# Image, text and weight loads of an early-fusion block: transfers cut at multiples of 16 rows, issued in another order, and the class row spread by transfers

## What is computed

```python
x = data.reshape(b, C, HP, P, WP, P).transpose(0, 2, 4, 1, 3, 5).reshape(b, N, F)   # 16, 36 patches, 768
x = jnp.einsum('bnf,df->bnd', x, W_lin) + b_lin
out = jnp.concatenate([cls, x], axis=1) + position_embeddings                        # 16, 37, 256
h = jnp.concatenate([out, txt], axis=1)                                              # 16, 165, 256
h = h + attn(layernorm(h), Wq, Wk, Wv, Wo)       # 16 heads, 4 key heads, rope, window of 32 to each side
h = h + ffn(layernorm(h), w1, conv_w, conv_b, w2)   # ternary weights, inputs rounded to 8 bits, conv of 3, silu
```

## Time and profile before

| | us |
|---|---|
| median of 3 runs | 399.28 |
| lowest, highest | 397.93, 400.9 |
| span of the profiled execution | 397.3 |
| PE busy in it | 364.4 |
| DVE busy | 306.3 |
| ACT busy | 256.9 |
| POOL busy | 215.4 |

### The profile page before, as it was taken

The page is one execution under the profiler, slowest core; times in us unless marked ns, Lnnn a source line. Parts: engine busy times, 40 slices in busy tenths (PEclk is TensorE's granted clock), DMA queues, the critical chain, the costliest instruction groups (busy, mean ns, idle before and its releaser), DMA issues.

```text
span 397.3 us, 8398 instructions
## 1 busy us (share of the span) xinstructions
PE 364.4 (92%) x3029; PEld 272.9 (69%) x3029; DVE 306.3 (77%) x647; ACT 256.9 (65%) x483; POOL 215.4 (54%) x245
## 2 busy tenths in 40 slices
PE   6599799999999999999989999999999998987885
PEld 2277557877877796678767876787678776843733
DVE  2247659654599889888998698959895997799795
ACT  3213436668786779567868686768677966772552
POOL 5406689689379919892789427972993016000000
PEclk9989999999999999999999999999999999999999
DMA  8781521201100022002000220022012001000101
GB/s 238 167 183 32 167 86 29 54 10 27 26 12 2 2 53 48 19 20 55 18 0 2 60 45 2 2 61 42 12 26 51 19 2 34 4 2 0 35 2 35
DMA packets 21907, 16.71 MB, mean 42 GB/s; under 512 B 12435, under 2 KB 20936, under 8 KB 21865
## 3 DMA queue, kind: packets, MB, share of 16 engines
q1 hardware_dynamic: 20970, 15.11, 15.4%
q10 hardware_dynamic: 895, 1.06, 1.0%
HBM read 9.82 MB, written 3.38 MB: 33 GB/s over the span
## 4 chain that ended last, share of the span: by engine, by line
PE 69%; DVE 14%; ACT 7%; issue 5%; DMA 4%; SPq 1%; DVEq 0%; ACTq 0%
PE bank L1790 8%; PE bank L1870 8%; PE bank L1841 7%; PE bank L1884 6%; PE bank L1943 5%; PE bank L1913 4%; PE bank L1984 4%; PE bank L1944 4%; DMA shared<-in_x 4%; PE bank L1861 4%; PE bank L1737 3%; PE bank L1904 2%; ACT shared L1339 2%; PE bank L1803 2%; PE bank L1893 2%
## 5 line engine op out<-in xcount | busy, mean ns | idle before, releaser
L1502 DVE TENSOR_REDUCE mx<-bank 120x4 fp32r<-120x376 f32 (+3 forms) x88 | 44.0, 506 | 24.5 <-PE bank L1853 24.1
L1274 ACT COPY pT<-bank 94x480 f32<-94x480 f32 (+3 forms) x88 | 48.2, 554 | 21.0 <-PE bank L1870 20.7
L1266 ACT ACTIVATE pr<-bank 120x376 f32<-120x376 f32 (+3 forms) x88 | 39.6, 454 | 28.9 <-PE bank L1861 28.1
L1870 PE MATMUL bank<-cst,pr 120*94 120x120 f32 (+3 forms) x352 | 51.3, 271 | 2.7 <-ACT pr L1266 2.7
L1841 PE MATMUL bank<-kbd,q_hl 128*120 128x376 f32 (+3 forms) x176 | 51.1, 373 | 1.2 <-ACT pT L1274 0.6
L1114 POOL TENSOR_TENSOR rs<-ve,half_neg 110x3 f32<-110x3 f32 x16 | 16.7, 1045 | 63.9 <-DVE ve L1530 47.7
L1943 PE MATMUL bank<-xT_hi,w1T 128*128 128x330 f32 x128 | 44.2, 351 | 1.3 <-DVE late L1585 0.9
L1870 PEld LDWEIGHTS bank<-cst,pr 120*94 120x94 f32 (+3 forms) x352 | 36.1, 122 | 10.4 <-ACT pr L1266 6.4
L1121 POOL TENSOR_SCALAR xn<-h,mv,rs 110x256 f32<-110x256 f32 x21 | 27.6, 1323 | 24.7 <-PE bank L1778 24.4
L1136 POOL TENSOR_TENSOR rc<-qk,cst 110x320 f32<-110x320 f32 x22 | 20.0, 909 | 38.3 <-ACT qk L1237 37.4
L1944 PE MATMUL bank<-xT_lo,w1T 128*128 128x330 f32 x128 | 39.5, 314 | 0.0
(11 more groups left out here) (132 smaller groups left out, 882.6 us busy)
## 6 DMA issues: line engine op xcount, KB each, us to landing
kbd<-shared SPq DMA_DIRECT2D x56, 41.2 KB, 2.1
out<-h SPq DMA_DIRECT2D x7, 330.0 KB
wn<-in_w SPq DMA_DIRECT2D x2, 1024.0 KB, 6.7
shared<-in_x SPq DMA_DIRECT2D x4, 432.0 KB
h<-in_txt SPq DMA_DIRECT2D x1, 770.0 KB
late<-in_lin SPq DMA_DIRECT2D x1, 768.0 KB, 7.1
vw<-v_rows SPq DMA_DIRECT2D x8, 94.0 KB
v_rows<-qk SPq DMA_DIRECT2D x8, 82.5 KB
```

The costliest lines, as they stand in the source:

```text
L1266: nc.scalar.activation(pr[:, g % 3, 0:HKV * WIDTH[j]], S_BANKS[g % 2][0:QP, 0:HKV * WIDTH[j]], ACT.Exp, scale=HD ** -0.5).then_inc(exped, 1)
L1274: nc.scalar.copy(pT[0:WIDTH[j], g % 3, :], S_BANKS[g % 2][0:WIDTH[j], 0:HKV * QP]).then_inc(p_kept, 1)
L1502: nc.vector.tensor_reduce(mx[:, g % 4, :].bitcast(F32R), S_BANKS[g % 2][0:QP, 0:HKV * WIDTH[j]].rearrange("p (k c) -> p k c", k=HKV), axis ...
L1870: o = nc.tensor.transpose(S_BANKS[g % 2][0:w, kv * QP:(kv + 1) * QP], pr[:, g % 3, kv * w:(kv + 1) * w], ident[0:QP, 0:QP])
```

## The change

Four edits.

1. Loads are cut at multiples of 16 rows. An image load becomes two transfers, of 64 and of 8 rows, and its two readers wait for both. The five pieces of text become eight: 64 + 9, 48 + 7, 16 + 2 and 96 + 14 rows.
2. SP issues image load 0, the patch weights, image loads 1 to 3, the text of pair 0, `wqk` and the mask; `wo` and `conv` follow the text of the other pairs. ACT's queue keeps the identity, the class row, the constants and the positions, in this order (positions were second).
3. POOL adds token and position once, for one row, in place in `clsb`. SP spreads the sum to the class rows of all pairs by two transfers with a repeated source, instead of one copy of `h` within `h`.
4. ACT sorts its half of image load 1 ahead of `keep_patch(0)`, no longer behind it.

```diff
--- before.py
+++ after.py
@@ -61,6 +61,7 @@
 LOADS = 4
 PER_LOAD = B // LOADS
 LROWS = PER_LOAD * CH * GRID
+EVEN_ROWS = LROWS // 16 * 16
 KP = CH * PATCH * PATCH // 128
 NTOK = B * NPATCH
 
@@ -740,7 +741,7 @@
     'dve.keep_pix_v': (3, 4, 8),
     'dve.abs_w': (19, 21),
     'dve.ternary': (24, 26, 29, 31, 32, 34),
-    'act.sort_a': (1, 3, 5),
+    'act.sort_a': (3, 5),
     'act.keep_pix_a': (2, 4, 10),
     'act.keep_patch': (6, 11, 26, 28),
     'act.keep_w': (59, 67, 73, 78),
@@ -978,13 +979,16 @@
         txt0 = 1 + NPATCH
         n00 = TT - txt0
         n10 = TT - first2 - txt0
-        TXT_PARTS = [
-            (txt0, txt0 + 64, 0, 0, 0),
-            (txt0 + 64, TT, 0, 0, 64),
+        TXT_RUNS = [
+            (txt0, TT, 0, 0, 0),
             (0, first2, 1, 0, n00),
             (first2 + txt0, TT, 1, 1, 0),
             (0, TT, 2, 1, n10),
         ]
+        TXT_PARTS = []
+        for p0, p1, t, b, r0 in TXT_RUNS:
+            even = p0 + (p1 - p0) // 16 * 16
+            TXT_PARTS += [(p0, even, t, b, r0), (even, p1, t, b, r0 + even - p0)]
 
         def sort_pix(i, lo, hi):
 
@@ -1003,8 +1007,7 @@
             eng.wait_ge(txt_first, 16 * len(TXT_PARTS))
             if n:
                 eng.wait_ge(txt_rest, 16 * len(TXT_PARTS))
-            eng.wait_ge(cls_made, 1)
-            eng.wait_ge(cls_moved, 16)
+            eng.wait_ge(cls_moved, 16 * 2)
             for s in tok_tiles(n):
                 eng.wait_ge(tok_in[s], 16 * len(tok_pieces(s)))
 
@@ -1015,14 +1018,17 @@
             xv = x.rearrange("b c (hp py) w -> (b c hp) (py w)", py=PATCH)
 
             def load_img(i):
-                sp.dma_start(raw[:, i, :], xv[LROWS * i:LROWS * (i + 1), :]).then_inc(img_in[i], 16)
+                for r0, r1 in ((0, EVEN_ROWS), (EVEN_ROWS, LROWS)):
+                    sp.dma_start(raw[r0:r1, i, :], xv[LROWS * i + r0:LROWS * i + r1, :]).then_inc(img_in[i], 16)
 
             load_img(0)
             sp.dma_start(wlT[:, :, :], lin_d).then_inc(wlin_in, 16)
+            for i in range(1, LOADS):
+                load_img(i)
             for p0, p1, t, b, r0 in TXT_PARTS:
                 sp.dma_start(h[p0:p1, 0, t, :], txt_v[b, r0:r0 + p1 - p0, 0, :]).then_inc(txt_first, 16)
-            for i in range(1, LOADS):
-                load_img(i)
+            sp.dma_start(wqk[:, :, :], wqk_d).then_inc(wqk_in, 16)
+            sp.dma_start(mask_sb[:, :], maskbits).then_inc(mask_in, 16)
 
 
             def move_tokens(s):
@@ -1036,10 +1042,13 @@
                 sp.dma_start(w2n[:, :, :], w2.rearrange("(t p) h -> p t h", p=128)).then_inc(w12_in, 16)
 
             sp.wait_ge(cls_made, 1)
-            sp.dma_start(h[first2:first2 + 1, :, 1, :], h[0:1, :, 0, :]).then_inc(cls_moved, 16)
+            for row, t in ((0, 0), (first2, 1)):
+                sp.dma_start(h[row:row + 1, :, t, :], clsb[:, 0:1, :].to_broadcast([1, PAIRS, D])).then_inc(cls_moved, 16)
             move_tokens(0)
             for p0, p1, t, b, r0 in TXT_PARTS:
                 sp.dma_start(h[p0:p1, 1:PAIRS, t, :], txt_v[b, r0:r0 + p1 - p0, 1:PAIRS, :]).then_inc(txt_rest, 16)
+            sp.dma_start(wo_sb[:, :, :], wo_d).then_inc(wts_in, 16)
+            sp.dma_start(conv[:, :, :], conv_d).then_inc(wts_in, 16)
 
             def load_v(n):
                 sp.wait_ge(v_ones, 1)
@@ -1103,8 +1112,7 @@
             nc.gpsimd.memset(ones[:, :], 1.0).then_inc(v_ones, 1)
             nc.gpsimd.memset(kbd[1][:, :, :, :], 0.0).then_inc(kbd_zeroed, 1)
             pool.wait_ge(cls_in, 16)
-            nc.gpsimd.tensor_tensor(h[0:1, :, 0, :], clsb[:, 0:1, :].to_broadcast([1, PAIRS, D]),
-                                    clsb[:, 1:2, :].to_broadcast([1, PAIRS, D]), ALU.add).then_inc(cls_made, 1)
+            nc.gpsimd.tensor_tensor(clsb[:, 0, :], clsb[:, 0, :], clsb[:, 1, :], ALU.add).then_inc(cls_made, 1)
             pool.wait_ge(consts_in, 16)
 
             def rstd(n, var, ve, rs, made, done):
@@ -1192,13 +1200,12 @@
         @block.scalar
         def _(act):
             act.dma_start(cst[:, 0:C_REST], ident_d).then_inc(ident_in, 16)
-            act.dma_start(posb[:, :], pos_d).then_inc(pos_in, 16)
             act.dma_start(clsb[:, :, :], cls_d).then_inc(cls_in, 16)
             act.dma_start(cst[:, C_REST:C_END], consts).then_inc(consts_in, 16)
-            act.dma_start(wqk[:, :, :], wqk_d).then_inc(wqk_in, 16)
+            act.dma_start(posb[:, :], pos_d).then_inc(pos_in, 16)
 
             def sort_pix_act(i):
-                act.wait_ge(img_in[i], 16)
+                act.wait_ge(img_in[i], 16 * 2)
                 if i >= 2:
                     act.wait_ge(pix_turned, 2 * (i - 1))
                 nc.scalar.copy(*sort_pix(i, GRID // 2, GRID)).then_inc(sorted_a, 1)
@@ -1216,11 +1223,9 @@
                     act.wait_ge(tok_in[s - 2], 16 * len(tok_pieces(s - 2)))
                 nc.scalar.copy(tokp[0:rows, s % 2, :], Z_BANKS[s % 2][0:rows, 0:D]).then_inc(tok_kept, 1)
 
-            act.dma_start(mask_sb[:, :], maskbits).then_inc(mask_in, 16)
-            act.dma_start(wo_sb[:, :, :], wo_d).then_inc(wts_in, 16)
-            act.dma_start(conv[:, :, :], conv_d).then_inc(wts_in, 16)
             sort_pix_act(0)
             keep_pix(0)
+            sort_pix_act(1)
             keep_patch(0)
 
             def keep_xn(n, k):
@@ -1381,7 +1386,7 @@
                 for s in work["keep_w"].get(q, ()):
                     keep_ternary(s)
                 for i in work["sort_a"].get(q, ()):
-                    sort_pix_act(i + 1)
+                    sort_pix_act(i + 2)
                 for i in work["keep_pix_a"].get(q, ()):
                     keep_pix(i + 1)
                 for s in work["keep_patch"].get(q, ()):
@@ -1396,7 +1401,7 @@
             nc.vector.tensor_scalar(neg_id[:, :].bitcast(F32R), ident[0:QP, 0:QP], -1.0, None,
                                     ALU.mult).then_inc(neg_made, 1)
             def sort_pix_dve(i):
-                dve.wait_ge(img_in[i], 16)
+                dve.wait_ge(img_in[i], 16 * 2)
                 if i >= 2:
                     dve.wait_ge(pix_turned, 2 * (i - 1))
                 nc.vector.tensor_copy(*sort_pix(i, 0, GRID // 2)).then_inc(sorted_v, 1)
```

## The result

The changed kernel takes 407.14 us (405.64 to 412.57, 4 runs) against 399.62 us (397.93 to 400.9, 4 runs): ratio 1.0158, 95% interval 1.0118 to 1.0198. It is slower by 1.6%: 6.3 us by the ratio, which leaves the slow execution of 412.57 us out, and 7.5 us by the two medians. The forecast was 2.5 us slower, in a range up to 404.6.

The account below looks back on a forecast made before the run. PE bounds the kernel, so only the start of its unbroken run at `turn_pix(2)` counts: +4.0 (positions) − 1.45 (image 2, sort) + 0 = +2.5 us on 399.28, giving 401.8 us, range 396.8 to 404.6.

Parts of the forecast that it names:

- Which wait decides: Start of `patch(0)`: set by the landing of the position rows in `posb`, 4.0 us later than before; chance 0.42.
- Records through at 6.0 us: ACT's queue on the positions' engine: 20 records after the identity already through, 29 left at 6.0 us.
- the 16.1 forecast: Landing of the position rows in `posb`, claimed at 16.1 us, with bounds of 12.9 and 17.3.
- 0.415 us an image row: Price of one image row on the positions' engine; 15 such rows and 18 ACT turns take 7.5 us, to 13.5.
- my own late bound of 0.55 for 16: Image rows at 0.55 us each on 16 engines, all to partitions 0 to 71; `posb` lands at 17.3 us.
- the case of the 72 partitions: Rival: partitions limit image loads, 1.2 us more than forecast: +3.7, 403.0 us, or 404.4 with a clock fall; chance 0.18.
- 6.85 us from `patch(0)` to `turn_pix(2)`: Distance between the two starts on PE once image 2 no longer binds: 6.85 us against 8.30 before.
- The clock as moved, at nothing: Half-clock stretch moves from `patch(1)` to the idle time ahead of `patch(0)`: +1.4 − 1.4 = 0, bound ±1.4 us.
- SP's queue hidden: Extra transfers on SP's queue are covered by waits for `tok_kept` and before `move_tokens(1)`: no time lost.
- the SP queue is late: Rival: tokens and rest-of-text behind more issues make `stats1_of(1)` late, 1 us more: 402.8 us; chance 0.08.
- Image 2 off the path, 1.45 us: Image 2 no longer holds `turn_pix(2)`; with ACT's earlier sort, a gain of 1.45 us at unchanged `patch(0)` start.
- The class row at nothing: POOL's add shrinks from 4.49 us to 0.6 to 1.2, SP issues two transfers instead of one: worth 0.

Follow-up runs that it names:

- second trace: The changed kernel run once more, unedited, for another trace: 407.55 us.
- the start mended: The changed kernel with positions loaded by two transfers of 32 and 5 rows, still last on ACT's queue: 399.27 us, ratio 0.9988 to the kernel before.
- the fastest kernel here: Changed kernel with 72-row images, constants and positions (32 + 5) behind weights on SP, pair 1's text and tokens first: 395.46 us, ratio 0.9854 to the kernel before.

## Why the prediction was right and wrong

- **Which wait decides: right.** `patch(0)` waits for the 37 position rows on one engine. Moving that one line costs 1.4% by itself, cutting it in two takes the loss away.
- **Records through at 6.0 us: the step that failed first.** I carried over 29 of 58 from the order of before. In the new order 20 were through, none of them a position row; 38 were left, not 29. The reading was wrong for the kernel before as well: of the 20 records that I put on that engine, 15 were position rows and 5 constants on other engines. Nor were the weights' rows through at 6.0: SP's queue had 153 records behind it, not the 214 of before, and the weights landed at 9.4 instead of 8.3 us, so image rows went until 16.3 us and not until 13.5. In return ten position rows passed between 6.8 and 8.0 us and the last ten between 16.1 and 17.3. `patch(0)` came 2.2 us later than the 16.1 forecast.
- **0.415 us an image row: too low.** It was 0.49. I had set the measured price of 12 engines against my own late bound of 0.55 for 16 and chosen the former. Total image traffic was 0.20 MB per us with 16 engines (0.81 MB in 4 us), against 0.21 with 12 (0.85 MB in 4 us, images as 72 rows), as the case of the 72 partitions had it. That agrees with the Trainium skill (SBUF — State Buffer, "Door 1: The DMA port swizzle"), by which partitions 0 to 63 reach half of the 16 ports.
- **6.85 us from `patch(0)` to `turn_pix(2)`: right but for the clock.** It was 8.41, of which 2.01 are the half clock; without it 6.40.
- **The clock as moved, at nothing: wrong.** At the start +2.0 − 1.4 = +0.6, inside the bound. The second fall, which I did not price, is 3.4 us longer, and 6.8 us longer in the changed kernel's second trace. In the first the distance grows from 5.5 to 6.5 us over it, in the second from 6.5 to 8.3. Why it lengthens was not settled.
- **SP's queue hidden: wrong.** This was the rival "the SP queue is late". The wait for tokens of pair 1 went from 0.86 to 4.15 us, of which 5.44 − 4.68 = 0.76 reached the first scores: PE waits 0.84 us for DVE at 48.21, where it did not before. With the start mended, putting text and tokens of pair 1 first gave the largest step in ratio of the orders tried (0.9988 to 0.9902), but its trace does not show by what.
- **Image 2 off the path, 1.45 us: right where positions are mended.** `turn_pix(2)` starts 6.4 us after `patch(0)` in those kernels too. But the division into 64 and 8 rows took 2.7 us back in the same stretch.
- **The class row at nothing: right.** POOL's add takes 0.71 us at 5.91 and SP waits afterwards; forecast was 0.6 to 1.2. Neither it nor ACT's earlier sort was undone by itself.

In the sum: +2.5 forecast, +2.2 positions, −0.4 distance, +0.6 clock at the start and +0.8 tokens give 5.7, where the trace has 5.4 at the first scores. With the 1.8 that the second fall adds in the second trace that is 7.5, the distance of the medians. That it comes out to the tenth is luck: `patch(0)` alone differed by 0.5 us between the two traces. The forecast's direction and first wait were right; its size was a third.

## What to carry to other kernels

Before a small transfer goes behind others, count on how many DMA engines its rows fall and which rows of the other queue they will alternate with; a few rows on one engine can hold a start that megabytes elsewhere do not. Put what gates the first product on one queue in the order of need, cut at a size that spreads over the engines, as in the fastest kernel here. And when a start moves earlier, follow it to the end of the trace: the next wait may take it back, on a queue, by the clock, or 200 us later.

## What was not expected of the hardware

- Dividing 72 rows on 12 engines into 64 on 16 and 8 on 8 delayed every later transfer of the queue: weights 7.5 instead of 6.4 us after an issue itself 0.7 us later, image 1 sorted from 17.21 instead of 13.38. 36 + 36 rows cost 0.85 us there (14.23) and nothing on the weights (5.8 us after issue). In the changed kernel the rate was 0.20 MB per us from 8 to 12 us with engines 100% busy, where with 12 engines it was 0.21 at 82%. That the first 8 engines, with 5 rows against 4, lag is consistent with this but was not shown engine by engine.
- Two queues on one engine shared it very differently by stretch: 37 rows of 1 KB in 2.3 us, with one gap of 0.3, when they were sent from 3.8 us on; 17 of them in 13 turns of 0.4 to 0.7 us between 8 and 16 us, in both traces of the changed kernel.
- A constants load of 132.5 KB landed from 4.4 to 10.1 us after issue, by what the other queue held (4.4 in the changed kernel, 10.1 with positions ahead of it, 9.7 beside undivided images).
